# Row fetches, soft routings, the two attention starts and the layer 1 experts of a four-layer gated kernel in a new order

## The reference

```python
x = x + tanh(g_xattn[0]) * L0_xattn(LN(x), itok, ctx)         # einsum("bsd,sod->bso", x, ctx[itok])
x = x + tanh(g_ffn[0])   * L0_ffn(LN(x), phi_w, phi_b, ...)   # soft routing to 64 experts x 32 slots
x = x + tanh(g_xattn[1]) * L1_xattn(LN(x), ctx, ctx, ...)     # rotary, causal, 16 heads of 8
x = x + tanh(g_ffn[1])   * L1_ffn(LN(x), ...)                 # 16 experts, top 2, plus a shared one
x = x + tanh(g_xattn[2]) * L2_xattn(LN(x), ctx, ctx)
x = x + tanh(g_ffn[2])   * L2_ffn(LN(x), ...)                 # experts choose 128 of 512 places
x = x + tanh(g_xattn[3]) * L3_xattn(LN(x), ctx, ctx, mask, ...)
x = x + tanh(g_ffn[3])   * L3_ffn(LN(x), ...)                 # 8 experts, top 2
```

```python
logits = (x @ phi_w.T + phi_b).reshape(t, z, 64, 32)
Dp = softmax(logits, axis=3);  C = softmax(logits, axis=2)
Xt = einsum('tznp,tzd->npd', Dp, x)
Xt = tanh((Xt - mean(Xt)) * rsqrt(var(Xt) + 1e-5))
Y  = einsum('tznp,npH->tzH', C, einsum('npd,ndH->npH', Xt, expert_w) + expert_b)
```

## Time and profile before

| what | value |
| --- | --- |
| median of 3 executions | 2147.64 us |
| lowest and highest | 2143.88 and 2164.28 us |
| the profiled execution | 2142.48 us, of which the span is 2140.7 us |
| granted clock of TensorE, mean over the span | 0.894 of full speed |
| busy share of the span | PE 80%, DVE 62%, ACT 56%, POOL 32% |

### The profile page before, as it was taken

How to read it: one execution, slowest core, us unless ns; L and a number is a source line. 1 busy time by engine, 2 the same in 40 slices (tenths; PEclk the granted TensorE clock), 3 DMA queues, 4 the chain that set the end, 5 groups by cost and what they waited for, 6 DMA issues and landing times. The chain is left out here.

```text
span 2140.7 us, 40008 instructions
## 1 busy us (share of the span) xinstructions
PE 1713.7 (80%) x12924; PEld 1252.7 (59%) x12924; DVE 1334.7 (62%) x3429; ACT 1188.4 (56%) x4072; POOL 683.0 (32%) x636
## 2 busy tenths in 40 slices
PE   3549999699999839999688865799649998649994
PEld 2425555377877616666487754545526676528883
DVE  4189999377777646667567757312446676674444
ACT  2149999178888618778544432334238888423333
POOL 3035555134444431212034421001300110156774
PEclk9879999599999969999899977799769999659997
DMA  3320000010000024333000022000033432301113
GB/s 109 71 99 1 1 0 1 17 35 1 1 0 1 17 63 109 77 90 100 25 1 0 0 79 83 3 0 0 6 93 95 99 88 68 125 12 46 50 52 138
DMA packets 49332, 99.25 MB, mean 46 GB/s; under 512 B 8842, under 2 KB 16332, under 8 KB 47556
## 3 DMA queue, kind: packets, MB, share of 16 engines
q1 hardware_dynamic: 44548, 87.68, 14.7%
q0 software_dynamic: 4608, 9.32, 1.4%
HBM read 68.14 MB, written 28.77 MB: 45 GB/s over the span
## 5 line engine op out<-in xcount | busy, mean ns | idle before, releaser
L585 ACT ACTIVATE B_E<-B_logits,B_m 128x32 f32<-128x32 f32 (+1 forms) x1792 | 360.2, 362 | 24.1 <-DVE B_m L554 22.6
L592 POOL TENSOR_TENSOR B_E<-B_E,B_r 128x512 f32<-128x512 f32 x256 | 267.7, 1046 | 316.8 <-DVE B_r L573 316.8
L1235 ACT ACTIVATE L_E<-L_sc,L_negm 128x128 f32<-128x128 f32 x1024 | 299.7, 405 | 122.2 <-DVE L_negm L1150 121.7
L1150 DVE TENSOR_REDUCE L_negm<-L_sc 128x4 f32<-128x512 f32 x256 | 174.2, 683 | 127.9 <-PE L_sc L1303 120.2
L554 DVE TENSOR_REDUCE B_m<-B_logits 128x16 f32<-128x512 f32 (+1 forms) x256 | 171.2, 669 | 56.5 <-PE B_logits L548 53.8
L1301 PE MATMUL L_sc<-KS,L_QS 128*128 128x512 f32 x256 | 142.0, 555 | 65.6 <-DMA L_QS<-L_qsplit 53.9
L568 DVE TENSOR_REDUCE B_r<-B_E 128x16 f32<-128x512 f32 (+1 forms) x256 | 172.8, 675 | 11.9 <-ACT B_E L585 10.1
L545 PE MATMUL B_logits<-B_phihi,B_xhi 128*128 128x512 f32 x256 | 156.2, 610 | 22.5 <-ACT B_E L585 10.6
L1243 ACT ACTIVATE L_PT<-L_pt 128x512 f32<-128x512 f32 x256 | 166.9, 654 | 0.6 <-PE L_pt L1311 0.6
L1311 PE MATMUL L_pt<-ident,L_E 128*128 128x128 f32 x1024 | 157.1, 276 | 1.6 <-ACT L_PT L1243 1.6
L1311 PEld LDWEIGHTS L_pt<-ident,L_E 128*128 128x128 f32 x1024 | 123.4, 142 | 24.1 <-ACT L_E L1235 2.0
(11 more groups left out here) (344 smaller groups left out, 3819.3 us busy)
## 6 DMA issues: line engine op xcount, KB each, us to landing
KS<-L_ksplit SPq DMA_DIRECT2D x192, 64.0 KB
L_QS<-L_qsplit SPq DMA_DIRECT2D x48, 256.0 KB, 3.9
F_w<-in_F_w SPq DMA_DIRECT2D x4, 2048.0 KB, 8.5
ew<-in_expert_w SPq DMA_DIRECT2D x1, 4096.0 KB, 14.6
L_cT<-in_ctxT SPq DMA_DIRECT2D x16, 256.0 KB, 4.7
L_ksplit<-L_khi SPq DMA_DIRECT2D x16, 256.0 KB, 2.0
L_ksplit<-L_klo SPq DMA_DIRECT2D x16, 256.0 KB, 2.4
L_qsplit<-L_qhi SPq DMA_DIRECT2D x16, 256.0 KB, 2.7
```

The source lines that it names most:

```text
L585: ins = nc.scalar.activation(e[:, cols], self.bank(w)[:, cols], ACT.Exp, bias=self.m[:, w % 4, g:g + 1])
L592: self.st.nc.gpsimd.tensor_tensor(e, e, self.r[:, w % 2, :].unsqueeze(2) .to_broadcast([128, self.ng, self.size]), ALU.mult).then_inc(self ...
L1150: nc.vector.tensor_reduce(negm[:, k % 4, :], sc[k % 2][:].rearrange("p (h k) -> p h k", h=NHG), AX.X, ALU.max, negate=True).then_inc(s["ma ...
L1235: ins = nc.scalar.activation(e[:, h * 128:(h + 1) * 128], sc[k % 2][:, h * 128:(h + 1) * 128], ACT.Exp, bias=negm[:, k % 4, h:h + 1])
```

## The change

**Stage A.** DVE clamps the indices to 0..31 and multiplies them by 128. PE then reads 16 at a time, and the inspection of each value is left out.

**Soft routings.** All loops are written out as one run over 128 units. Banks are taken in turn, unit k in bank k mod 3 (B1 before: 0, 1, 0, 2). The normalisation of the next group is spread, one operation after each of four units, and B2's end of the group before is spread over four units too. B2 gets 3 banks, 8 buffers, sums two units behind, and turns four units behind instead of three. B2's bias multiplication goes away. Instead feature 0 of the normalised input is set to 1, row 0 of phiT[1] is set to the bias, and the old row 0 is subtracted from every row of phiT[1]. This is exact since the features of a normalised token sum to zero. The subtraction is new work of POOL in stage Mid: a row of DRAM is read into all 128 partitions of `bc` (1 MB), then come a clearing and four subtractions. One set of bias parts is left, for B1.

**Attention starts.** The clearing of QS goes to POOL, behind the split of Q. The clearing of OZ and VZ[0] goes behind DVE's work on Q, that of VZ[1] behind the taking of V. For group 0, ACT's queue issues the transfers of Q.

**Layer 1 experts.** DVE keeps 4 of the 16 experts (3, 7, 11, 15), ACT and POOL get 12. There are 3 banks and 6 buffers for these 12. The shared expert comes after the first three experts. The computation of the weights is cut into two parts (`choose` and `weigh`), and the turn of the weights is put at the end of a group.

The diff, cut to its core:

```diff
@@ stage_a @@
-            t.wait_ge(s["tok_in"], 16)
+            t.wait_ge(s["tok_ready"], 1)
...
-            for h in range(S // 8):
-                _, toks = nc.values_load_multi_w_load_instructions(itok[0:1, 8 * h:8 * h + 8], engines=[mybir.EngineType.PE],
-                                                                   min_val=0, max_val=B - 1)
+            for h in range(S // 16):
+                _, rows = nc.values_load_multi_w_load_instructions(
+                    itoc[0:1, 16 * h:16 * h + 16], engines=[mybir.EngineType.PE], min_val=0, max_val=(B - 1) * D,
+                    skip_runtime_bounds_check_because="VectorE has clamped them")
@@ SoftUnit @@
+    def bank(self, k):
+        return self.banks[k % len(self.banks)]
...
+    def tensor_logits(self, eng, k, x, p):
+        q, bank, last = k % NQ, self.bank(k)[:], k - len(self.banks)
+        nc, cols = self.st.nc, slice(q * 512, (q + 1) * 512)
+        if last >= 0 and self.shifted(last):
+            eng.wait_ge(self.diff_done, self.shifts(last))
+        elif last >= 0:
+            eng.wait_ge(self.exp_done, last + 1)
...
-        nc.tensor.matmul(bank, p.ones16[:], self.bias3[:, cols], start=False, stop=True).then_inc(self.logits_ready, 1)
+        ins = nc.tensor.matmul(bank, xhi, self.lo[:, cols], start=False, stop=self.bias3 is None)
+        if self.bias3 is not None:
+            ins = nc.tensor.matmul(bank, p.ones16[:], self.bias3[:, cols], start=False, stop=True)
+        ins.then_inc(self.logits_ready, 1)
@@ stage_mid @@
             sp.dma_start(sel[:], d["sel_expert"]).then_inc(ew_in, 16)
+            sp.dma_start(bc[:], d["phiT_slots"][0:1, :].to_broadcast([128, NE_L0])).then_inc(bc_in, 16)
+            sp.dma_start(p.phiT[1][0:1, :], d["phi_b_slots"]).then_inc(bias_row_in, 16)
 
         @block.gpsimd
         def _(g):
+            g.wait_ge(bc_in, 16)
+            nc.gpsimd.memset(bc[0:1, :], 0.0).then_inc(row_set, 1)
+            g.wait_ge(row_set, 1)
+            g.wait_ge(bias_row_in, 16)
+            for q in range(4):
+                cols = slice(q * 512, (q + 1) * 512)
+                nc.gpsimd.tensor_tensor(p.phiT[1][:, cols], p.phiT[1][:, cols], bc[:, cols], ALU.subtract)
             g.wait_ge(var_ready, 1)
             nc.gpsimd.tensor_tensor(rs[:], mv[:, :, 1], p.mhalf[:, 0:NC], ALU.pow).then_inc(rs_ready, 1)
@@ stage_b2 @@
-        soft = SoftUnit(st, NL, ct_ready, p.phiT[1], p.bias3[1], 4)
+        soft = SoftUnit(st, NL, ct_ready, p.phiT[1], None, 4, 8, DELAY, 3)
@@ stage_attn, vector @@
             normalise(0)
-            for u in range(2):
-                nc.vector.memset(VZ[u][:], 0.0).then_inc(s["VZ_zeroed"], 1)
-                nc.vector.memset(QS[u][3 * HW:128, :, :].bitcast(F32), 0.0).then_inc(s["QS_zeroed"], 1)
-            steps.link(nc.vector.memset(OZ[:], 0.0))
-            nc.vector.memset(diagonal(OZ[:], OZ[:].offset), 1.0)
...
@@ stage_attn, scalar @@
             upper("q", 0)
+            a.wait_ge(s["q_split"], 1)
+            for i, part in enumerate((hi["q"], lo["q"])):
+                a.dma_start(split_d["q"][0][i], part[:].bitcast(F32)).then_inc(s["q_put"], 16)
+            a.wait_ge(s["q_put"], 32)
+            spread_q(a, 0)
@@ stage_l1_ffn @@
-    NO = NR // 2
+    NO, NA, RP, SH = NR // 4, NR - NR // 4, 6, 3
...
+                own(n, u, k, 0)
+                if not first:
+                    finish(n - 1, 1 - u)
+                own(n, u, k, 1)
+                if more:
+                    rt.choose(v, n + 1, steps)
+                own(n, u, k, 2)
+                if more:
+                    rt.weigh(v, n + 1, 1 - u, steps)
+                own(n, u, k, 3)
```

More of the change, by code:

```diff
@@ L532, in vector_split @@
             .then_inc(self.phi_split, 1)
[L534 to L542 removed]
+    def tensor_logits(self, eng, k, x, p):
[5 more added lines that the diff above has]
+            eng.wait_ge(self.exp_done, last + 1)
+        if k < NQ:
             eng.wait_ge(self.phi_split, q + 1)
@@ L602, in stage_b1 @@
     LAG, DELAY = 5, 2
+    NU = NG * UG
     with Stage(nc, "B1") as st:
@@ L622, in _ @@
             credit(g, (soft.probs_ready, 2))
-            over_groups_skewed(g, lambda n, u, first, more: [soft.gpsimd(g, n * UG + w, w) for w in range(UG)])
+            for k in range(NU):
+                soft.gpsimd(g, k)
         @block.vector
@@ L814, in _ @@
             credit(g, (soft.probs_ready, 2))
-            def group(n, u, first, more):
-                for w in range(UG):
-                    soft.gpsimd(g, n * UG + w, w)
-                    if w == 10 and not first:
-                        tail.gpsimd(g, n - 1, 1 - u)
-            over_groups_skewed(g, group)
+            for k in range(NU):
+                soft.gpsimd(g, k)
+                if k % UG == 13 and k > UG:
+                    tail.gpsimd(g, k // UG - 1, (k // UG - 1) % 2)
             tail.gpsimd(g, NG - 1, 1)
@@ L857, in _ @@
+            for k in range(NU - DELAY, NU):
+                soft.vector_sum(v, k)
+                soft.vector_inverse(v, k)
+            steps.need(add(NG - 1))
+            tail.vector(v, NG - 1, 1, steps, None)
         @block.scalar
@@ L932 @@
+            for k in range(NU, NU + LAG + 1):
+                if k < NU + LAG:
+                    turn(k - LAG)
+                combine(k - LAG - 1)
 NHG = 4
```

477 lines of the change are left out of this document (243 added, 234 removed).

## The result

The changed kernel takes 2013.36 us (median of 4 runs, 2011.66 to 2021.61), the kernel before beside it 2150.22 us. The ratio is 0.9352, with a 95% interval of 0.9315 to 0.9389. That is 6.5% faster. The forecast was 2053 us, with a range of 2020 to 2092, so the kernel came out 40 us under the forecast. The profiled execution has a span of 2009.9 us against 2140.7, so 130.8 us are to be found.

The account below looks back on a forecast made before the run. The prediction took DVE to bound B1 and PE to bound steady B2, with PE idling in stage A, the attention starts and F1. Its terms summed to −94 us, from 2147.6 to 2053.6, called 2053 us, range 2020 to 2092.

Parts of the forecast that it names:

- B2, −24: Soft routing stage B2: dropping the bias multiplication brings a unit to 2.09 us, −24 us (−10 to −34).
- Rival 2: B2 becomes bound by ACT, a unit settling at 2.2 us; with stage A gaining only 12, 2079 us; chance 0.13.
- Stage A, −24: Gather of stage A: half the loads and no inspections cut PE's idle time, −24 us (−10 to −30).
- a sign of being wrong: Stage A: loads of 16 values taking much over 0.6 us would show the forecast wrong.
- Mid, +7: Stage Mid: transfer, clearing and subtractions ahead of POOL's inverse roots delay them, +7 us (+2 to +14).
- B1, −3: Stage B1: DVE stays the bound and only its gaps can go, −3 us (+6 to −9).
- F1, −28: Layer 1 experts: DVE's smaller share removes PE's idle time, 19.5 us a group, −28 us (−10 to −40).
- Rival 1: F1 stays bound by elementwise engines, DVE and POOL contending for memory: −8 instead of −28, 2073 us; chance 0.15.
- the −13 and −9: Attention starts: moved clearings and Q on ACT's queue give −13 us in layer 1, −9 us in layer 3.
- the prediction's sign for "gives nothing": Layer 1 attention: scores no less than 29 us after PE's first multiplication would mean Q's own queue gives nothing.
- Rival 3: All stages: PE idles less, its clock reaches 1.00 in F1 and the gather; −120 us, 2027 us; chance 0.14.
- Rival 4: B2: PE pauses in every unit and TensorE's clock falls; 2176 us at 60 slow units; chance 0.03.

## Why the prediction was wrong

The direction was right, and so was what bounds each stage, B1 aside. Four terms missed on the same side, and three of them, A, Mid and B2, lie beyond the ranges given for them.

**B2, −24 against −42.8, start and end included: the step that failed.** It took the pace before from one unit, 2.28 us of the earlier trace rows, and the pace after as 2.09 us, for fear that ACT had "little room". The pace before was 2.38: about one unit in six took 2.7 to 3.7 us, and PE waited 10.6 us in all for ACT's exponentials. One picked unit does not show this, though the earlier trace rows has PE idle for 2 of 40 us. The pace after was PE's work alone, 2.04 us. The runs split the gain into 29.6 us for the multiplication, whose full price the prediction had (29.4) and then cut, and 14.5 for the rotation, which it priced at nothing. Rival 2, ACT as the bound, fell: ACT was busy 37.34 of 40 us and PE waited for it almost nowhere.

**Stage A, −24 against −34.9.** The mechanism was right, and the run with the inspections shows that it was these alone. The prediction called the idle time of 30.2 us the most it could give. That was no bound: PE's own work also fell, from 38.3 to 30.7 us, as the clock in the gather rose from 0.89 to 1.00. (Some 5 of the 30.2 us also lie ahead of the first multiplication: within the gather PE idled 63.6 − 38.3 = 25.3 us.) The stretch up to the gather became 2.2 us shorter, so the clamping on DVE cost nothing that shows. The loads of 16 values took 1.1 to 2.1 us, not 0.6. The prediction named this as a sign of being wrong, but with 3.0 us of waits for "issue" in all, most of their time was hidden. The Trainium skill's 200 ns for a register of a load ("Runtime: NRT & Kernel Launch", instruction fetch mechanics) would be 3.2 us for 16 values, an estimate; the loads measured here, from on-chip memory, are below it.

**Mid, +7 against −1.8.** The mechanism and its size were right: the roots started 359.47 − 340.36 = 19.1 us after the stage's first copy, and before 393.35 − 380.86 = 12.5 us, so 6.6 us late. What came on top was the experts' clock. Their 16 rounds took 12 us at 1.00 instead of 20 at 0.50. In 17 profiles of kernels with a changed Mid this happened in 8. In 3 profiles of kernels with Mid as before it never did. With the clock down, Mid takes 50.5 to 51.0 us, and 44.1 + 6.6 = 50.7 is just that. So the full clock in Mid, some 8 us in both profiles of the table, was luck, and no sign of the prediction's mechanism.

**B1, −3 against −5.7.** The gaps became rarer, as forecast. But the bound was read off wrongly: PE is busy for 236.67 us in the earlier trace rows, DVE for 234.80, and with the change PE is busy for 98% of the stage and DVE for 94%.

**F1, −28 against −34.8.** Most of PE's idle time of 3.2 us a group went, as forecast; 0.7 us is left. The clock's part was counted in words and hardly in the sum: a group's granted clock rose from 0.93 to 1.00. A group takes 18.6 us, 0.9 less than forecast. The prediction reckoned the gain from the split alone. The runs show that the order alone is a loss, and that the split is one when the shared expert comes first right behind the turn. Rival 1, contention between POOL and DVE, was wrong in its price. L1566 takes 682 ns, not more than the 1020 of the earlier trace rows, since it no longer falls together with an addition on POOL. But DVE's normalisation (L123) does, and takes 736 ns instead of 341: 1.6 us more a group by the means, for which PE never waited. The rule of the Trainium skill ("GPSIMD Engine Reference", key points), that the two share memory interfaces, with contention when DVE reads two inputs or runs in a mode with two ports, is borne out where the runs put them side by side: the slots' normalisation of stage Mid, 9.4 us instead of 4.2. Which of the two cases the normalisation is, with its one tensor input, no trace tells. The rival had the right mechanism, but not where it costs time.

**The attentions.** Their starts came out at −11.2 and −7.0, close to the −13 and −9. The clearing's 9.4 us measured 9.7. Q's own queue gave 1.5 us, not 3.5: the prediction's sign for "gives nothing", 29 us from PE's first multiplication to the scores, was nearly met at 27.7. The 7.8 us lost behind the first scores were not foreseen. In both kernels PE waits up to 3 us at the start of a group for Q's transfer, 8.0 us in all before and 14.1 us with the change, which is most of the loss. But this stretch strayed from 264.7 to 287.7 us among runs of the changed attention. Whether the change has a part in it stays open.

Rival 3, the terms at their far ends (2027), was the nearest, with a chance of 0.14, and it named the clock rising to 1.00 in F1 and the gather. Rival 4, the clock falling in B2, did not come: PE stayed the bound there, and its clock stayed at 1.00.

## What to carry to other kernels

Take the pace of a loop from its first and last turn over the whole stage, never from one turn: the waits that a new rotation of buffers removes are in the mean alone. Where PE pauses and its clock reads under 1.00, removing the pauses gives the idle time and the slower work behind them, so idle time is no upper bound. Two parts of a change can give a gain only together, as the split and the order of F1 did, so an undo of one part says nothing on what that part would do alone.
